# Attention kernel on one core: the chunk mask as two ScalarE copies ahead of the scores, layer 0's output bias in 32-column tiles and added behind the maximum

## The chip, the core and the metric

One core of a Trainium2 chip runs the whole program. Its engines are named as in the profile: PE (TensorE, matmuls), DVE (VectorE), ACT (ScalarE), POOL (GpSimd) and SP (SyncE, which issues the DMAs). PE reads weights and moving data from SBUF and writes PSUM. PE's granted clock was 0.996 of full speed (2.4 GHz) in the profiled execution. The metric is the device time of the program in microseconds, the median of three runs.

## What is computed

Sixteen samples, each 256 channels by 2048 positions, go through two attention layers. `ctx` is y below.

```python
# layer 0: 8 heads of 32 channels; scores over positions, 32x32 for each head
q, k, v = Wq @ y + bq, Wk @ y + bk, Wv @ x + bv
attn = softmax(einsum('bhdl,bhel->bhde', q, k) / 16)
o = Wo @ einsum('bhde,bhel->bhdl', attn, v) + bo + x
x1 = group_norm(o) * gn_w + gn_b          # one mean and variance for each sample
# layer 1: q, k, v from y; chunks of 64 positions, 8 heads
s = einsum('bnqhd,bnkhd->bnhqk', qh, kh) / sqrt(32)
s = s + where(mask_of_key > 0, 0, -1e9)
out = (softmax(s) @ vh) @ W_out.T + b_out
z = out.transpose * mask + x1
return (z - mean) * rsqrt(var + eps)      # over positions, for each channel
```

Layer 0 never forms q, k and v: the kernel builds the Gram matrix of y, from it the scores and the attention, and folds the attention and the weights into one 256x256 matrix M (with the identity added for the residual) and one bias of 256 values. Then o = M x + bias.

## The kernel before

**Slots and units.** A sample is cut in 4 blocks of 512 positions; a block in 4 slots, so a sample has 16 slots s = 0 to 15, with b, j = divmod(s, 4) and u, e = divmod(s, 2). A unit u (0 to 7) is 256 positions, four chunks. Every engine has its own instruction stream, written out by hand in a `body(n, first, last)` that runs over the slots; semaphores alone tie them together. The last sample leaves the loop after slot 11 and has a hand-written tail on PE, ACT and DVE.

**Layer 1.** In each slot PE makes projections of the next block out of y split in a high and a low part (three matmul passes of 128x512 or 128x256 columns, `three_pass`, L313): q and k in slots j = 0 and 1, v in j = 2 and 3. In an even slot `scores(n, u)` writes the unit's scores into `s_ps` (two PSUM banks, one unit deep). It begins with four mask matmuls of 32 rows and 512 columns (L326), which multiply `blocked` (1 where a key is masked, bf16, from `flags` on DVE, L835) with `neg_rows` (-1e9 over the scale, in three bf16 pieces) and open the accumulation, and goes on with 32 small matmuls in 32x64 tiles (L337). DVE takes the maximum (`top`, L839) and subtracts it (`shift`, L846), ACT takes the exponents (L650), DVE sums (L851) and inverts, POOL scales the probabilities (L1125), PE transposes them (L348) in the next two slots, ACT copies that out (L645), and two units later (`LAG` = 2) PE multiplies with v (`values`, L366). ACT casts the result to `att_hi` (L668), DVE makes `att_lo` (L863), PE applies W_out, DVE adds the branch's bias and mask (`branch`, L868). The scores of a unit wait until the `shift` before them has emptied `s_ps`.

**Layer 0.** Slots 1 to 4 build the Gram matrix (`gram_part`, L433), 5 to 8 turn it into scores: `copy_hl` and `copy_lower` on ACT, `L441` to `L465` on PE, the column tiles of L459 and L465 being 32 wide. Slot 10 (`S_U`): DVE normalizes, PE makes U (L471), ACT's `copy_u0` (L707) copies it out after the exponents. Slot 11 (`S_M`): PE makes M (L477) and, on the whole array, the bias W bv (L480, 128x128 weights, one column); DVE adds the identity (L903), splits M in m_hi and m_lo (L905, L907) and adds bo to the bias (L908). In slots 12 to 15 (`S_MX`) PE makes o for a block of x in two halves of six matmuls (`layer0_output`, L313 into `l_ps`), ACT copies each half out with the bias (`copy_output`, L683), DVE takes statistics (L915). x is split by ACT and DVE one slot earlier (`split_x`, L623 and L829), from slot 11 on.

**The sample before.** Its normalization runs under the next sample: ACT's `group_normed` (L658), POOL's `join` (L1142), DVE's statistics and `result` (L994, in slots 10 to 13), SP's stores.

**Order within DVE's slots.** For slots 11 and 12 it is: branch, sums, split_x, result, the three instructions of M, o_bias; then branch, top, att_low, shift. The PE stream of slot 12 is scores(6), values(4), the output of block 0, the projections.

**SP** loads x, y, yt and the mask two to three slots ahead of their use, each load behind a wait until its buffer is free.

## Time and profile before

| | |
|---|---|
| median of three runs | 1559.06 us (1558.3 to 1560.88) |
| profiled execution | 1557.83 us, its span 1556.0 us |
| PE busy | 1527.3 us, 98% |
| DVE busy | 1324.1 us, 85% |
| ACT busy | 999.5 us, 64% |
| POOL busy | 451.4 us, 29% |
| q1, all loads and stores | 32.0% of 16 DMA engines |
| granted clock of PE | 0.996 |

The profile comes from one execution. A group of instructions is named by its line, engine, operation and tiles, out <- in, with shapes; the page's groups give busy time and the mean of one. In a timeline each row is a start, a duration and an instruction; what stands in brackets is the idle time of that engine ahead of it and who ended it. Instructions of one engine overlap a little, so the cost of one is best read from start to start. The chain of work that ended last is followed backwards from the last instruction through whatever released each step. All times of a timeline are microseconds from the start of the span.

### The profile page before, as it was taken

The numbers are of one execution on the slowest core, as the hardware profiler recorded it, in microseconds if no ns is written. First come the engines' busy times: TensorE is split into PE (matmuls) and PEld (weight loads), VectorE is DVE, ScalarE is ACT, GpSimd is POOL, SyncE is SP. The second block draws the span as 40 slices with busy tenths as digits, with TensorE's granted clock in tenths as the row PEclk, the third lists the DMA queues.
The fourth block names the chain that finished last, engine by engine and source line by source line (L and its number), as shares of the span: only waits on it lengthen the run. The fifth ranks groups of instructions, "written<-read, shape, count | busy, mean of one in ns | idle before, by whom it ended". The sixth has DMA issues, their size and how long they took to land.

```text
span 1556.0 us, 55525 instructions
## 1 busy us (share of the span) xinstructions
PE 1527.3 (98%) x24660; PEld 1287.2 (83%) x24660; DVE 1324.1 (85%) x2028; ACT 999.5 (64%) x1808; POOL 451.4 (29%) x294
## 2 busy tenths in 40 slices
PE   9999999999999999999999999999999999999995
PEld 7888888888888888888888888888888888888874
DVE  5778888888898888988888888888888889898897
ACT  5656665666656667566575665766666665666655
POOL 1114133141331414214142241423314133141331
PEclk9999999999999999999999999999999999999998
DMA  7132331424324242241433415234142331424221
GB/s 256 54 96 77 110 123 41 145 84 117 110 67 133 70 142 86 83 123 63 143 83 103 124 45 151 88 98 123 49 150 79 120 111 55 133 82 127 59 72 67
DMA packets 96399, 157.33 MB, mean 101 GB/s; under 512 B 5408, under 2 KB 38304, under 8 KB 96032
## 3 DMA queue, kind: packets, MB, share of 16 engines
q1 hardware_dynamic: 96160, 153.78, 32.0%
q8 instruction: 195, 3.19, 0.9%
q14 instruction: 44, 0.36, 0.1%
HBM read 120.20 MB, written 33.55 MB: 99 GB/s over the span
## 4 chain that ended last, share of the span: by engine, by line
PE 86%; DVE 12%; issue 1%; ACT 1%; POOL 0%; ACTq 0%; POOLq 0%; DVEq 0%
PE pj_ps L313 41%; PE l_ps L313 12%; PE l_ps L433 7%; PE s_ps L337 7%; PE w_ps L348 7%; PE w_ps L366 6%; DVE o_sb L994 3%; PE s_ps L326 2%; PE l_ps L450 2%; DVE row_sum L851 1%; DVE prob L846 1%; DVE x_lo L829 1%; DVE y_lo L820 1%; DVE u_sb L868 1%; DVE m_lo L907 1%
## 5 line engine op out<-in xcount | busy, mean ns | idle before, releaser
L1125 POOL TENSOR_TENSOR prob<-prob,row_inv 128x1024 f32<-128x1024 f32 x128 | 258.3, 2018 | 903.8 <-DVE row_inv L856 903.8
L668 ACT CAST att_hi<-w_ps 128x256 fp32r<-128x256 f32 x256 | 82.9, 376 | 227.4 <-PE w_ps L366 221.0
L313 PE MATMUL pj_ps<-y_hi,w_hi 128*128 128x512 f32 x510 | 206.8, 405 | 0.0
L313 PE MATMUL pj_ps<-y_hi,w_lo 128*128 128x512 f32 x510 | 201.3, 395 | 0.0
L313 PE MATMUL pj_ps<-y_lo,w_hi 128*128 128x512 f32 x510 | 201.2, 394 | 0.0
L851 DVE TENSOR_REDUCE row_sum<-prob 128x16 f32<-128x1024 f32 x128 | 154.9, 1210 | 52.1 <-ACT prob L650 52.1
L839 DVE TENSOR_REDUCE row_max<-s_ps 128x16 f32<-128x1024 f32 x128 | 155.9, 1218 | 33.7 <-PE s_ps L337 31.1
L645 ACT COPY prob_t<-w_ps 128x512 f32<-128x512 f32 x256 | 149.8, 586 | 14.2 <-PE w_ps L348 11.4
L1142 POOL TENSOR_TENSOR o_sb<-o_sb,u_sb 128x1024 f32<-128x1024 f32 x60 | 157.9, 2642 | 2.6 <-ACT o_sb L658 2.6
L824 DVE TENSOR_TENSOR yt_hl<-yt_raw,yt_hl 128x1024 fp32r<-128x1024 f32 x64 | 119.8, 1872 | 42.7 <-ACT yt_hl L613 40.8
L846 DVE TENSOR_TENSOR prob<-s_ps,row_max 128x1024 f32<-128x1024 f32 x128 | 155.4, 1214 | 0.1
L313 PE MATMUL pj_ps<-w_hi,y_hi 128*128 128x256 f32 x512 | 150.3, 294 | 0.7 <-ACT v_s L641 0.7
L348 PE MATMUL w_ps<-cst,prob 128*128 128x128 f32 x1024 | 147.6, 275 | 1.8 <-DVE att_lo L863 1.8
L337 PEld LDWEIGHTS s_ps<-k_s,q_s 32*64 32x64 f32 x8192 | 140.7, 133 | 9.5
L630 ACT ACTIVATE q_s<-pj_ps,col 128x512 f32<-128x512 f32 x128 | 88.3, 690 | 88.0 <-PE pj_ps L313 87.1
L313 PE MATMUL pj_ps<-w_hi,y_lo 128*128 128x256 f32 x512 | 144.6, 282 | 0.0
L313 PE MATMUL pj_ps<-w_lo,y_hi 128*128 128x256 f32 x512 | 144.0, 281 | 0.0
L683 ACT ACTIVATE o_sb<-l_ps,o_bias 128x512 f32<-128x512 f32 x128 | 88.7, 693 | 86.2 <-PE l_ps L313 86.1
L337 PE MATMUL s_ps<-k_s,q_s 32*64 32x64 f32 x8192 | 140.7, 217 | 0.0
L650 ACT ACTIVATE prob<-prob 128x1024 f32<-128x1024 f32 x128 | 137.3, 1072 | 4.7 <-DVE prob L846 4.7
L348 PEld LDWEIGHTS w_ps<-cst,prob 128*128 128x128 f32 x1024 | 118.8, 141 | 24.1 <-issue 10.4
L829 DVE TENSOR_TENSOR x_lo<-x_raw,x_hi 128x1024 fp32r<-128x1024 f32 x62 | 82.2, 1325 | 59.1 <-ACT x_hi L623 59.0
(141 smaller groups left out, 3540.0 us busy)
## 6 DMA issues: line engine op xcount, KB each, us to landing
y_raw<-in_ctx SPq DMA_DIRECT2D x64, 512.0 KB, 4.8
yt_raw<-in_ctx_t SPq DMA_DIRECT2D x64, 512.0 KB, 4.8
x_raw<-in_x SPq DMA_DIRECT2D x64, 512.0 KB, 5.3
out_z<-o_sb SPq DMA_DIRECT2D x60, 512.0 KB, 3.6
mask_b<-in_mask SPq DMA_DIRECT2D x64, 256.0 KB, 4.0
out_z<-o_sb SPq DMA_DIRECT2D x8, 256.0 KB, 2.6
u_sb<-in_w SPq DMA_DIRECT2D x2, 512.0 KB, 5.8
w_sb<-in_w SPq DMA_DIRECT2D x1, 1024.0 KB, 11.1
```

What stands on the lines that cost most here:

```text
L313: last = mm(dst, lhs, rhs, start=i == 0, stop=i == len(todo) - 1)
L337: last = mm(s_ps[64 * h:64 * h + 64, r, t // 2, g, t % 2, :], q_s[rows, b % 2, g, cut], k_s[rows, b % 2, g, cut], start=False, stop=t == 3 ...
L348: last = nc.tensor.transpose(pt_ps[:, j, 2 * g + r, :], prob[:, u % 2, r, j, g, :], ident)
L433: last = mm(l0_ps[i][:, i * P:], yt_hl[:, lb, 0, i * P:(i + 1) * P], hi_lo[:, i * P:], start=q == 0 and lb == 0, stop=q == BLOCKS - 1 and ...
L645: copy(prob_t[:, j].rearrange("p g r h q -> p (g r h q)"), w_ps[:, j, :]).then_inc(pt_copied, 1)
L650: nc.scalar.activation(cut, cut, ACT.Exp, scale=SCALE1).then_inc(exp_done, 1)
L824: tt(yt_hl[:, :, 1, :], yt_raw[:, q % 2], yt_hl[:, :, 0, :], ALU.subtract).then_inc(yt_lo_done, 1)
L839: nc.vector.tensor_reduce(row_max[:, u % 2, :], s_ps[:, :, :, :, :, :].rearrange("p r j g c k -> p (r j g c) k"), AX.X, ALU.max).then_inc( ...
L846: tt(prob[:, u % 2].rearrange("p r j g (c k) -> p (r j g c) k", c=2), s_ps[:, :, :, :, :, :].rearrange("p r j g c k -> p (r j g c) k"), ro ...
L851: nc.vector.tensor_reduce(row_sum[:, u % 2, :], prob[:, u % 2].rearrange("p r j g (c k) -> p (r j g c) k", c=2), AX.X, ALU.add).then_inc(s ...
L1125: nc.gpsimd.tensor_tensor(cut, cut, row_inv[:, u % 2, :].unsqueeze(2).to_broadcast([P, 2 * HEADS, CHUNK]), ALU.mult).then_inc(probs_done, 1)
L1142: nc.gpsimd.tensor_tensor(o_sb[:, :, cut], o_sb[:, :, cut], u_sb[:, :, cut], ALU.add).then_inc(z_done, 1)
```

## The change

The mask matmuls go. `blocked` becomes f32 and holds -1e9 over the scale (or 0) itself; before each unit ACT copies it, spread over the heads, into both banks of `s_ps` (`preset_mask`), and all score matmuls add to what stands there. A copy for unit u + 1 is issued right behind the exponents of unit u and waits for the shift of unit u; PE's scores wait for it. Five zero matmuls instead of six at the start write all of `s_ps` once.

On ACT `copy_lower` moves from slot 7 to slot 6 and `copy_u0` within slot 10, both ahead of the exponents.

Layer 0's bias leaves slot 11: `layer0_bias` makes it as sixteen matmuls in 32-column tiles behind `values(n, 4)` in slot 12, and DVE's `output_bias` adds bo right behind `top(n, 6)`. PE waits for it only ahead of the second half of block 0's output, ACT ahead of its first copy. DVE does the three instructions of M in slot 11 ahead of `result`. In the last sample SP loads x one slot earlier, and DVE's tail takes `top`, the bias and `att_low` ahead of `split_x(n, 1)`.

The diff, without the lines that only declare or drop semaphores and `neg_rows`:

```diff
@@ -96,7 +95,7 @@
         v_s = sb("v_s", [P, 2, PAIRS, E])
-        blocked = sb("blocked", [P, 2, BT], BF16)
+        blocked = sb("blocked", [P, 2, BT])
...
@@ -274,6 +272,8 @@
                         q = s - start + 2
+                        if last and load == load_x:
+                            q += 1
                         if 2 <= q < 6 and not (last and q >= 4):
...
@@ -317,16 +317,7 @@
                     pe.wait_ge(qkv_copied, count(n, 24, 6 * b + 3))
-                    pe.wait_ge(blocked_done, count(n, 4, b))
-                if exists(n, 8, u - 1):
-                    pe.wait_ge(shifted, count(n, 8, u - 1))
-                for i in range(4):
-                    r, h = divmod(i, 2)
-                    rows = slice(DH * i, DH * i + DH)
-                    mm(s_ps[64 * h:64 * h + 64, r].rearrange("p j g c k -> p j g (c k)"), neg_rows[rows, :],
-                       blocked[rows, b % 2, e * UT:(e + 1) * UT].rearrange("p (j t) -> p j t", j=2).unsqueeze(2).to_broadcast([DH, 2, HALVES, P]),
-                       start=True, stop=False)
-
+                pe.wait_ge(mask_set, count(n, 8, u))
...
@@ -335,7 +326,7 @@
                             last = mm(s_ps[64 * h:64 * h + 64, r, t // 2, g, t % 2, :], q_s[rows, b % 2, g, cut], k_s[rows, b % 2, g, cut],
-                                      start=False, stop=t == 3 and g == HALVES - 1)
+                                      start=False, stop=True, skip_group_check=True)
                 last.then_inc(scores_ready, 1)
...
@@ -474,19 +465,27 @@
                         for i in range(HALVES):
-                            mm(l0_ps[0][:, k * E:(k + 1) * E], w0_sb[:, V_W, i, k * P:(k + 1) * P], u0[:, i, :], start=i == 0, stop=i == 1)
-                    for k in range(HALVES):
-                        for i in range(HALVES):
-                            last = mm(l0_ps[1][:, k:k + 1], u0[:, i, k * P:(k + 1) * P], col[:, V_BV0, i:i + 1], start=i == 0, stop=i == 1)
+                            last = mm(l0_ps[0][:, k * E:(k + 1) * E], w0_sb[:, V_W, i, k * P:(k + 1) * P], u0[:, i, :], start=i == 0, stop=i == 1)
                     last.then_inc(m_ready, 1)
+
+            def layer0_bias(n):
+
+                pe.wait_ge(u0_copied, count(n, 1, 0))
+                for k in range(HALVES):
+                    for i in range(HALVES):
+                        for h in range(4):
+                            last = mm(l0_ps[1][DH * h:DH * h + DH, k:k + 1], u0[:, i, k * P + DH * h:k * P + DH * h + DH], col[:, V_BV0, i:i + 1],
+                                      start=i == 0, stop=i == 1)
+                last.then_inc(bias_ready, 1)
...
                     pe.wait_ge(m_lo_done, count(n, 1, 0))
-                    pe.wait_ge(o_bias_done, count(n, 1, 0))
                 for o in range(HALVES):
+                    if q == 0 and o == 1:
+                        pe.wait_ge(o_bias_done, count(n, 1, 0))
                     if exists(n, 8, 2 * q + o - 2):
...
@@ -503,10 +502,9 @@
             zeros = prob[:, 0].rearrange("p r j g m -> p (r j g m)")[:, 0:512]
-            for i in range(6):
+            for i in range(5):
                 last = mm(s_ps[:, i % 2].rearrange("p j g c k -> p (j g c k)"), zeros[:, 0:P], zeros, start=True, stop=True)
             last.then_inc(banks_open, 1)
-            pe.wait_ge(banks_open, 1)
             pe.wait_ge(w_hi_done, 1)
...
@@ -536,6 +533,8 @@
                             values(n, u - LAG)
+                    if s == S_MX:
+                        layer0_bias(n)
                     if s == 0 and not first:
...
@@ -563,6 +562,7 @@
             values(n, 4)
+            layer0_bias(n)
             layer0_output(n, 0)
...
@@ -649,6 +649,19 @@
+            def preset_mask(n, u):
+                b, e = divmod(u, 2)
+                if e == 0:
+                    act.wait_ge(blocked_done, count(n, 4, b))
+                if exists(n, 8, u - 1):
+                    act.wait_ge(shifted, count(n, 8, u - 1))
+                else:
+                    act.wait_ge(banks_open, 1)
+                for r in range(2):
+                    last = copy(s_ps[:, r].rearrange("p j g c k -> p j g (c k)"),
+                                blocked[:, b % 2, e * UT:(e + 1) * UT].rearrange("p (j t) -> p j t", j=2).unsqueeze(2).to_broadcast([P, 2, HALVES, P]))
+                last.then_inc(mask_set, 1)
+
             def group_normed(n, q):
...
@@ -678,6 +691,8 @@
                     act.wait_ge(stored[q], count(n - 1, 1, 0, 16))
+                if q == 0:
+                    act.wait_ge(o_bias_done, count(n, 1, 0))
                 for o in halves:
...
@@ -719,6 +734,7 @@
                 copy_k(0, 0, g)
+            preset_mask(0, 0)
             for m in range(2):
...
@@ -740,8 +756,6 @@
                         copy_hl(n)
-                    if s == S_SUM + 1:
-                        copy_lower(n)
                     if s == S_SC + 1:
...
@@ -758,12 +772,15 @@
                         copy_pt(n, u - 1, 0)
+                    if s == S_SUM:
+                        copy_lower(n)
+                    if s == S_U:
+                        copy_u0(n)
                     if e == 0:
                         exponents(n, u)
+                        preset_mask(n, u + 1)
                     if j == 1 and not (last and b + 2 >= BLOCKS):
                         split_y(n, b + 2)
-                    if s == S_U:
-                        copy_u0(n)
                     if not first and s in (2, 3):
...
@@ -785,6 +802,7 @@
             copy_output(n, 1)
+            preset_mask(n, 7)
             split_x(n, 3)
...
@@ -831,8 +849,8 @@
                 if exists(n, 8, 2 * (b - 2) + 1):
-                    dve.wait_ge(scores_ready, count(n, 8, 2 * (b - 2) + 1))
-                nc.vector.tensor_scalar(blocked[:, b % 2, :], mask_b[:, b % 4, :], 0.0, None, ALU.is_le).then_inc(blocked_done, 1)
+                    dve.wait_ge(mask_set, count(n, 8, 2 * (b - 2) + 1))
+                nc.vector.tensor_scalar(blocked[:, b % 2, :], mask_b[:, b % 4, :], 0.0, NEG / SCALE1, ALU.is_le, ALU.mult).then_inc(blocked_done, 1)
...
@@ -905,7 +923,6 @@
                     tt(m_lo[:, :, :], m_t[:, :, :], m_hi[:, :, :], ALU.subtract).then_inc(m_lo_done, 1)
-                    tt(o_bias[:, :], l0_ps[1][:, 0:HALVES], col[:, V_BO0, :], ALU.add).then_inc(o_bias_done, 1)
                 elif S_MX <= s < S_MX + BLOCKS:
...
@@ -913,6 +930,10 @@
                     nc.vector.bn_stats(o_stats[:, HALVES * q + o, :], o_sb[:, o, q * BT:(q + 1) * BT]).then_inc(o_stats_done, 1)
+
+            def output_bias(n):
+                dve.wait_ge(bias_ready, count(n, 1, 0))
+                tt(o_bias[:, :], l0_ps[1][:, 0:HALVES], col[:, V_BO0, :], ALU.add).then_inc(o_bias_done, 1)
...
@@ -1024,6 +1041,8 @@
                         top(n, u)
+                        if s == S_MX:
+                            output_bias(n)
                         if not (first and u < LAG):
...
@@ -1053,11 +1072,14 @@
                         instance_norm(n - 1)
+                    if s == S_M:
+                        layer0(n, s)
                     if not first and T_FINAL <= s < T_FINAL + BLOCKS:
...
                         layer0_inverse(n)
-                    layer0(n, s)
+                    if s != S_M:
+                        layer0(n, s)
                     if s == SLOTS - 1 and not last:
...
@@ -1066,10 +1088,11 @@
             branch(n, 1, 1)
+            top(n, 6)
+            output_bias(n)
+            att_low(n, 4)
             split_x(n, 1)
-            top(n, 6)
             shift(n, 6)
-            att_low(n, 4)
             split_x(n, 2)
```

## Rows read from the trace of the kernel before

**Rows 1.** Page of the profile: busy time and share by engine; the chain that ended last.

```profile
PE 1527.3 (98%) x24660; PEld 1287.2 (83%) x24660; DVE 1324.1 (85%) x2028; ACT 999.5 (64%) x1808; POOL 451.4 (29%) x294
...
PE 86%; DVE 12%; issue 1%; ACT 1%; POOL 0%; ACTq 0%; POOLq 0%; DVEq 0%
```

**Rows 2.** List of waits: engine, what waited <- releaser: us in total, times, longest.

```profile
PE l_ps L313 <- DVE o_bias L908: 6.3, 14, 0.6
```

**Rows 3.** Timeline of PE, sample 7, slots 11 and 12: start us, us, engine, line.

```profile
744.48 0.95 PE L480 MATMUL l_ps<-col,work_b 128*128 128x1 f32 x8
...
745.29 0.48 PE L313 MATMUL pj_ps<-att_hi,w_hi 128*128 128x512 f32 x1
...
746.86 0.41 PE L326 MATMUL s_ps<-blocked,neg_rows 32*64 32x512 bf16 x4
...
747.10 1.10 PE L337 MATMUL s_ps<-k_s,q_s 32*64 32x64 f32 x64
...
749.59 0.47 PE L313 MATMUL l_ps<-x_hi,m_hi 128*128 128x512 f32 x1 [0.60 <-DVE o_bias L908]
```

**Rows 4.** Groups of ACT by line and shape: busy us, mean ns | idle before.

```profile
L645 ACT COPY prob_t<-w_ps 128x512 f32<-128x512 f32 x256 | 149.8, 586 | 14.2 <-PE w_ps L348 11.4
...
L658 ACT ACTIVATE o_sb<-o_sb,gn 128x512 f32<-128x512 f32 x120 | 91.4, 815 | 0.0
```

**Rows 5.** Timeline of ACT, slots 5, 6, 9 and 10 of sample 7; [idle before it].

```profile
713.83 0.69 ACT L634 ACTIVATE k_s<-pj_ps,col 128x512 f32<-128x512 f32 x1 [0.47 <-PE pj_ps L313]
...
716.22 0.65 ACT L668 CAST att_hi<-w_ps 128x256 fp32r<-128x256 f32 x2 [0.48 <-PE w_ps L366]
...
734.47 0.69 ACT L634 ACTIVATE k_s<-pj_ps,col 128x512 f32<-128x512 f32 x1 [0.53 <-PE pj_ps L313]
...
736.53 0.65 ACT L668 CAST att_hi<-w_ps 128x256 fp32r<-128x256 f32 x2
```

**Rows 6.** Timeline of DVE and GpSimd (POOL), slots 11 and 12 of sample 7.

```profile
743.65 1.16 DVE L829 TENSOR_TENSOR x_lo<-x_raw,x_hi 128x1024 fp32r<-128x1024 f32 x1
...
743.82 2.75 POOL L1125 TENSOR_TENSOR prob<-prob,row_inv 128x1024 f32<-128x1024 f32 x1 [7.80 <-DVE row_inv L856]
...
744.73 2.58 DVE L994 TENSOR_SCALAR o_sb<-o_sb,z_rstd,z_shift 128x512 f32<-128x512 f32 x2
...
747.23 0.68 DVE L903 TENSOR_TENSOR work_a<-l_ps,cst 128x512 f32<-128x512 f32 x1
...
747.94 0.43 DVE L905 CAST m_hi<-work_a 128x512 fp32r<-128x512 f32 x1
...
749.08 0.74 DVE L868 SCALAR_TENSOR_TENSOR u_sb<-pj_ps,c,mask_b 128x512 f32<-128x512 f32 x1
...
750.87 0.74 DVE L863 TENSOR_TENSOR att_lo<-w_ps,att_hi 128x256 fp32r<-128x256 f32 x2
...
755.74 1.00 DVE L994 TENSOR_SCALAR o_sb<-o_sb,z_rstd,z_shift 128x512 f32<-128x512 f32 x2
```

**Rows 7.** GpSimd's scaling on the page's groups; an x_lo of slot 13, timeline of DVE.

```profile
L1125 POOL TENSOR_TENSOR prob<-prob,row_inv 128x1024 f32<-128x1024 f32 x128 | 258.3, 2018 | 903.8 <-DVE row_inv L856 903.8
...
760.68 1.72 DVE L829 TENSOR_TENSOR x_lo<-x_raw,x_hi 128x1024 fp32r<-128x1024 f32 x1 [1.34 <-ACT x_hi L623]
```

**Rows 8.** Chain in order of time, slot 8: start us, us, what.

```profile
730.37 0.39 PE l_ps L459 x32
```

**Rows 9.** Timeline of PE and ACT, slots 10 and 11 of sample 7.

```profile
738.57 1.10 PE L471 MATMUL l_ps<-w_sb,a_wide 128*128 128x256 f32 x4
...
739.65 1.06 ACT L650 ACTIVATE prob<-prob 128x1024 f32<-128x1024 f32 x1 [0.29 <-DVE prob L846]
...
742.01 1.05 ACT L623 CAST x_hi<-x_raw 128x1024 fp32r<-128x1024 f32 x1
```

**Rows 10.** Chain at the start of the span; timeline of ACT in the last sample.

```profile
1.31 7.07 PE s_ps L507 x12
...
1515.33 1.05 ACT L623 CAST y_hi<-x_raw 128x1024 fp32r<-128x1024 f32 x1 [3.39 <-DMA x_raw<-in_x]
```

More of the change, by code:

```diff
@@ L152, in build @@
         wqk_in, wvo_in, cols_in, consts_in, w0_in = sem("wqk_in"), sem("wvo_in"), sem("cols_in"), sem("consts_in"), sem("w0_in")
-        neg_done = sem("neg_done")
-        zeros_set, banks_open = sem("zeros_set"), sem("banks_open")
+        zeros_set, banks_open, mask_set = sem("zeros_set"), sem("banks_open"), sem("mask_set")
         consts_done = sem("consts_done")
@@ L1004, in _ @@
             flags(0, 0)
-            dve.wait_ge(consts_in, 16)
-            for i in range(4):
-                last = nc.vector.tensor_copy(neg_rows[DH * i:DH * i + DH, :], cst[0:DH, C_NEG:C_NEG + CHUNK])
-            last.then_inc(neg_done, 1)
             split_y(0, 1)
```

4 lines of the change are left out of this document (1 added, 3 removed).

## Prediction

> **What bounds the kernel now.** I began with the page: TensorE (PE) is busy for 98% of the span, VectorE (DVE) for 85%, ScalarE (ACT) for 64%, and the chain that ended last runs 86% on PE and 12% on DVE [rows 1]. So what leaves PE comes off the time, except where PE waits. Then the list of waits: in the steady state one wait of PE is left, 0.45 us in each of 14 samples, the first matmul of layer 0's output for the bias (`o_bias`) [rows 2]. Then sample 7 in order of time (one sample takes 95.3 us): before that matmul PE stood 0.60 us [rows 3], and DVE had worked without a break since slot 10. So slots 10 to 12 are set by DVE, all others by PE. I name stretches by their slot, units 0 to 7 by their scores; all times are those of sample 7.
>
> **The mask leaves PE.** Each unit has four mask matmuls, which start at 746.86; the scores behind them start at 747.10 [rows 3]. That is 0.24 us. The chain of PE shows 0.34 for them, since it counts the 0.1 us gap ahead of them too, which is a change of tile size and stays when the scores follow the projections directly. The first weights of the scores, now hidden under the mask, may come into the open; that takes up to 0.07. I take 0.24 us a unit, bounds 0.17 and 0.34.
>
> **Two ACT copies a unit take its place.** The trace has no ACT copy from SBUF to PSUM. The nearest is the copy of 128x512 out of PSUM, 586 ns; the dearest form with 512 columns takes 815 ns [rows 4]. Back to back ACT instructions overlap by about 0.1, so a pair costs 0.96 us, bounds 0.9 and 1.45. In all 128 pairs, 123 us, put ACT at 73% of the span. The pair stands behind the exponents, a whole unit (about 12 us) ahead of its scores, so the scores don't wait for it; what it delays is ACT's queue behind it: the transposed copy, the split of x or yt, k's copies, split_y, and `att_hi`, for which att_lo on DVE and then PE's transposes wait. ACT's idle time takes this up in most slots. Two places are tight. Slots 5 and 6: 0.47 us of idle before k's second copy and 0.48 before `att_hi` just hold a pair [rows 5], but not PE's new earliness too, so unit 3 gains 0.17 instead of 0.24. Slots 9 and 10: 0.53 before k and none before `att_hi` [rows 5], so `att_hi` comes when it came before, and unit 5's mask gives nothing.
>
> The other units: the mean over partitions in slot 0 waits for DVE's aggregate, which comes within 0.3 us of PE now, so unit 0 gains 0.10. Units 7, 1, 2 and 4 gain 0.24 each. Sum: 0.96 + 0.17 + 0.10 = 1.23 us a sample; unit 6 belongs to the next part. The flags now write f32 with a second operation, same columns; DVE has that time.
>
> **Slots 10 to 12, the order of DVE.** Today x_lo is followed by result (2.50 us for two), the sum of M (0.71), m_hi, m_lo and o_bias, which ends at 749.16; PE starts the output at 749.59 and its second half 1.39 later, at 750.98 (half of a group of 2.79) [rows 3, 6]. Result is that slow because GpSimd's scaling of the probabilities came in at 743.82, behind x_lo, and took 2.75 us [rows 6]. The mean over all 128 is 2.02, about 17 of them long, so 1.91 for the others [rows 7]. It and these DVE instructions exclude each other: two results cost 0.91 (755.74 to 756.65) where GpSimd rests, and an x_lo started under a running scaling took 1.72 instead of 1.16 [rows 6, 7].
> After: x_lo leaves DVE at 744.73. The sum of M reads PSUM and runs under the scaling, its input ready at once, since the bias matmuls are no longer ahead of the signal. m_hi, at 745.44, copies from SBUF to SBUF at the speed of a result (0.43 and 0.46 for 512 columns), not of a sum (0.6 to 0.7), so I take it as held as the result was, until the scaling ends at 746.57, and done at 746.78. Then m_lo 0.61 (747.39), two results at their free cost 0.91 (748.30), branch and maximum 1.79 (750.09) [rows 6], and only then o_bias, done at 750.24. m_lo comes in time. The bias comes 1.08 us later than before, because branch and maximum now stand ahead of it, but it is wanted 1.39 later.
> PE on its side: the bias matmuls on the whole array took 0.81 (744.48 to 745.29) [rows 3]; as 32-column tiles they resemble the 32 small ones of y's sums, 0.39 for all [rows 8]; with 0.24 for unit 6, PE would start the output at 748.28 and reach its second half at 749.67. There it waits for o_bias: 750.24 and 0.1 to 0.42 of restart. So the second half starts at 750.34 to 750.66 instead of 750.98, and the bias, the mask and the old wait, worth 1.3 together, give 0.3 to 0.6. I take 0.5. Sum for a sample: 1.73 us.
>
> **x_hi and the port.** copy_u0 is moved ahead of the exponents. Its matmuls end at 739.67 [rows 9], so: copy at 739.71, exponents at 740.18 (before: 739.65), pair at 741.14, transposed copy 742.10, x_hi at 742.58 against 742.01 [rows 9], done at 743.62. x_lo may then start at 743.65, when it starts now, and 0.17 ahead of the scaling. That is the thinnest margin of the change.
> The Trainium skill, SBUF — State Buffer, section Who interferes with whom, says that the first to issue gets the pair of ports shared by DVE and GpSimd for its whole instruction and that the other is blocked; the rows of the scaling agree, and by that rule a pair 0.2 us dearer turns the order round, which is the first rival.
> The Trainium skill, ScalarE: Activation LUTs, gives an ACTIVATE without pointer operands 186 ns + 0.833 ns an element, from which I estimate 0.61 us, and also says that writing to PSUM is quicker than to SBUF; no row here shows it. By 0.61 x_lo starts at 743.71, by a quicker write earlier, ahead of GpSimd in both, and the sum stays.
>
> copy_lower, one slot earlier, finds its transpose done; 0.27 us ahead of exponents that have slack. Ends: PE's chain begins with twelve records (six matmuls) of zeros up to 8.38 us [rows 10]; five end near 7.5 and the weights at 7.91 take over: 0.45, and 0.24 for unit 0. In the last sample ACT stands 3.39 us for x [rows 10]; that load moves one slot ahead on SP's queue, in front of a store, and att_low comes before split_x, but DVE is nearly full there: 1.6, bounds 0 and 2.7.
>
> **Sum.** 15 x 1.73 = 26.0, 0.7 and 1.6: 28.3 us. Profiled execution 1557.83 - 28.3 = 1529.5 (span 1527.7); the median of the three runs lies 1.23 above it, so 1530.8.
>
> **Rivals.**
> (a) GpSimd gets in first. If the pair costs over about 1.15 us, x_lo starts after 743.82, is blocked to 745.73 and leaves DVE at 746.81; then 0.71, 0.46, 0.61, 0.91, 1.79 and 0.15 put o_bias at 751.44, 1.20 later than forecast. 16 x 1.20 = 19: 1550. For: the margin of 0.17. Against: ACT's copies are regular (586 ns on average over 256).
> (b) The bias isn't late. If the cast isn't held by GpSimd, m_lo is done at 746.5, the first result is held as it is now, and o_bias is done at 749.17, 1.07 earlier; PE never waits: 0.81 more a sample, 1518; with masks at 0.34, 1511. For: the sum of the sizes that leave PE. Against: the held result of the same speed [rows 6].
> (c) Slower: the write into PSUM is dear. If a copy of 512 columns costs as much as the longest ACT instruction, 1.06 us for the exponents of 1024 [rows 9], a pair takes 1.93, 0.97 more. It then comes out whole in slots 5 and 6 and again in 9 and 10, and (a) besides: 1.73 - 0.97 - 0.97 - 1.20 = -1.4 us a sample, 1578 with the ends. It turns slower from a pair of about 1.3 us, where (a)'s 1.20 and twice 0.34 have used up 1.73 and the ends; at 815 ns a copy it would be 1564. No row speaks for it but the lack of one; ACT's copies cost 0.82 ns a column whatever the form.
> (d) PE's gain is used up by small waits at many places (ACT and DVE are both fuller): nothing is left, 1558.
>
> **How the numbers follow.** Forecast 0.43, (a) 0.24, (b) 0.20, (c) 0.08, (d) 0.05. The time is the forecast's. The range leaves out (c), (d) and the outermost of (b): 1510 to 1552. A measurement of this kernel can tell 0.2%, about 3 us, from no change. Faster: forecast, (a) and (b), 0.87; same 0.05; slower 0.08.
>
> **What would show it.** Line 326 gone, ACT near 73% with copies into `s_ps` of 0.56 to 0.62 us; in every sample x_lo of slot 11 at 1.16 us and GpSimd's scaling there at 2.75 (forecast), or x_lo over 2 us and the scaling at 1.91 (a); PE idle about 0.7 to 1 us ahead of the second half of the output's first block, released by o_bias. (b) is shown by no such wait and m_hi at 0.43. The period of a sample should be 93.5 us. The forecast is wrong if a new wait on `att_hi` or on line 915's copies appears in PE's list, or if the score matmuls themselves become longer.

## The result, and the profile of the changed kernel

The changed kernel takes 1548.17 us, median of 4 runs (1545.97 to 1549.55), against 1559.15 for the kernel before (4 runs): ratio 0.9924, 95% interval 0.9912 to 0.9936. It is 11 us faster. The forecast said 28 us faster, 1530.8. The sign was right and the time lies in the range, but the size was wrong by a factor of 2.5. Its profiled execution took 1545.97 us with a span of 1544.2, so 11.8 of the span's 1556.0 us went.

The page's busy times and its chain, to be read beside [rows 1]:

```profile
PE 1506.1 (98%) x24530; PEld 1264.6 (82%) x24530; DVE 1287.5 (83%) x2024; ACT 1109.2 (72%) x2064; POOL 451.0 (29%) x294
...
PE 78%; DVE 12%; ACT 7%; issue 2%; DMA 0%; ACTq 0%; POOL 0%; SPq 0%; POOLq 0%; DVEq 0%
```

PE lost 21 us of busy time, the span only 11.8. ACT is at 72% (forecast: near 73) and now has 7% of the chain, where it had 1%. "issue" has 2%, where it had 1%: time in which PE stood although the profile shows nothing that it waited for. PE's list of waits (us in total, times, longest), the answer to [rows 2]:

```profile
PE l_ps L313 <- DVE o_bias L936: 9.3, 13, 0.9
...
PE w_ps L357 <- issue: 2.8, 5, 1.0
...
PE l_ps L477 <- issue: 1.5, 2, 1.2
```

The wait for the bias did not go, it grew from 6.3 to 9.3 us, as the forecast had it (it stands ahead of the second half now). The other two rows have no counterpart in the kernel before, and the forecast has no term for them. PE in slots 11 and 12 of sample 7, to be read beside [rows 3]:

```profile
740.67 1.16 PE L328 MATMUL s_ps<-k_s,q_s 32*64 32x64 f32 x64
...
742.55 0.43 PE L477 MATMUL l_ps<-col,work_b 128*32 128x1 f32 x32
742.91 0.50 PE L313 MATMUL l_ps<-x_hi,m_hi 128*128 128x512 f32 x1
...
745.26 0.50 PE L313 MATMUL l_ps<-x_hi,m_hi 128*128 128x512 f32 x1 [0.69 <-DVE o_bias L936]
```

The line of the mask is gone; the 32 small bias matmuls take 0.36 (742.55 to 742.91; forecast 0.39); the second half stands 0.69 us for `o_bias` (forecast 0.7 to 1). But the scores take 1.16 us instead of 1.10. DVE and GpSimd in the same stretch, beside [rows 6]:

```profile
738.44 1.23 DVE L847 TENSOR_TENSOR x_lo<-x_raw,x_hi 128x1024 fp32r<-128x1024 f32 x1
739.58 0.68 DVE L921 TENSOR_TENSOR work_a<-l_ps,cst 128x512 f32<-128x512 f32 x1
740.30 1.41 DVE L923 CAST m_hi<-work_a 128x512 fp32r<-128x512 f32 x1
741.74 0.69 DVE L925 TENSOR_TENSOR m_lo<-work_a,m_hi 128x512 fp32r<-128x512 f32 x1
742.35 1.00 DVE L1015 TENSOR_SCALAR o_sb<-o_sb,z_rstd,z_shift 128x512 f32<-128x512 f32 x2
743.26 0.74 DVE L886 SCALAR_TENSOR_TENSOR u_sb<-pj_ps,c,mask_b 128x512 f32<-128x512 f32 x1
743.93 1.21 DVE L857 TENSOR_REDUCE row_max<-s_ps 128x16 f32<-128x1024 f32 x1
745.06 0.15 DVE L936 TENSOR_TENSOR o_bias<-l_ps,col 128x2 f32<-128x2 f32 x1
```

```profile
738.51 2.91 POOL L1148 TENSOR_TENSOR prob<-prob,row_inv 128x1024 f32<-128x1024 f32 x1 [7.61 <-DVE row_inv L874]
```

This is the order that the forecast worked out: x_lo gets in ahead of GpSimd (by 0.07 us; 0.17 before), the sum of M (`work_a`) runs under the scaling, `m_hi` is held until the scaling ends (1.41 instead of 0.43), and the two results take 1.00, as they do where GpSimd rests [rows 6]. In samples 0 and 15 alone GpSimd came first and x_lo took 2.58.

To see where the time went I took the starts of the score matmuls of all 128 units. The table has the distance from one unit's start to the next, less the same distance in the kernel before, as the median of samples 1 to 14: a negative number is time won. "0 to 1" is the stretch from unit 0's scores to unit 1's. The columns are the kernels of this document (e1 to e7 are the experiments below); "forecast" is that of the prediction.

```
us          forecast  after    e1     e2     e3     e4     e5     e6     e7
0 to 1        -0.24   -0.16  -0.17  -0.16   0.00  -0.15  -0.15  -0.15  -0.15
1 to 2        -0.24   -0.15  -0.17  -0.15   0.00  -0.15  -0.15  -0.15  -0.15
2 to 3        -0.17   -0.19  -0.19  -0.19   0.00  -0.19  -0.20  -0.20  +0.99
3 to 4        -0.24   -0.12  -0.18  -0.13  +0.01  -0.12  -0.12  -0.12  +0.06
4 to 5         0.00   -0.04  -0.03  -0.01  +0.01  -0.04  -0.03  -0.03  -0.04
5 to 6                -1.05  -0.17  -0.17  -0.89  -1.06  -1.07  -1.07  -0.90
6 to 7                +0.73   0.00  +0.21  +0.55  -0.24  +1.32  +1.56  +1.55
5 to 7        -0.74   -0.32  -0.17  +0.04  -0.34  -1.30  +0.25  +0.49  +0.65
7 to next 0   -0.10   -0.18  -0.18  -0.18   0.00  -0.18  -0.22  -0.22  -0.22
sum           -1.73   -1.16  -1.08  -0.78  -0.33  -2.13  -0.62  -0.38  +1.15
```

(Sums are those of the unrounded medians.) A second mark, from the start of unit 5's scores to the first matmul behind block 0 of the output in slot 12 (below: the end of the block), shows the DVE stretch by itself: 17.64 us before, 17.54 after (medians of samples 1 to 14). It gave 0.10, where the forecast took 0.5.

### The profile page after: what moved, and what is told of

The parts are those of the page before. It is cut to its first block, busy times and chain, and to the rows that moved or that the text cites. A ratio compares the mean times of both kernels' runs of the same rounds, so it can differ in the third digit from the quotient of the medians.

```text
span 1544.2 us, 55594 instructions
## 1 busy us (share of the span) xinstructions
PE 1506.1 (98%) x24530; PEld 1264.6 (82%) x24530; DVE 1287.5 (83%) x2024; ACT 1109.2 (72%) x2064; POOL 451.0 (29%) x294
## 3 DMA queue, kind: packets, MB, share of 16 engines
q8 instruction: 194, 3.18, 0.9%
## 4 chain that ended last, share of the span: by engine, by line
PE 78%; DVE 12%; ACT 7%; issue 2%; DMA 0%; ACTq 0%; POOL 0%; SPq 0%; POOLq 0%; DVEq 0%
PE pj_ps L313 39%; PE l_ps L313 10%; PE l_ps L424 7%; PE s_ps L328 7%; PE w_ps L339 6%; PE w_ps L357 5%; PE l_ps L441 2%; DVE x_lo L847 1%; DVE o_sb L1015 1%; DVE row_max L857 1%; DVE m_hi L923 1%; DVE prob L864 1%; ACT s_ps L661 1%; ACT prob L650 1%; DVE row_sum L869 1%
## 5 line engine op out<-in xcount | busy, mean ns | idle before, releaser
L328 PEld LDWEIGHTS s_ps<-k_s,q_s 32*64 32x64 f32 x8192 | 130.8, 133 | 43.1 <-issue 35.0
L842 DVE TENSOR_TENSOR yt_hl<-yt_raw,yt_hl 128x1024 fp32r<-128x1024 f32 x64 | 94.9, 1483 | 70.0 <-ACT yt_hl L613 70.0
L328 PE MATMUL s_ps<-k_s,q_s 32*64 32x64 f32 x8192 | 148.5, 220 | 0.0
L661 ACT COPY s_ps<-blocked 128x512 f32<-128x512 f32 x256 | 143.1, 603 | 0.0
```

The costliest lines, as they stand in the source:

```text
L328: last = mm(s_ps[64 * h:64 * h + 64, r, t // 2, g, t % 2, :], q_s[rows, b % 2, g, cut], k_s[rows, b % 2, g, cut], start=False, stop=True, ...
L661: last = copy(s_ps[:, r].rearrange("p j g c k -> p j g (c k)"), blocked[:, b % 2, e * UT:(e + 1) * UT].rearrange("p (j t) -> p j t", j=2). ...
```

## The experiments

All are timed in 5 rounds beside the kernel before, which took 1559.8 to 1560.6 us in those rounds.

### One part alone

**e1_nomask**: the kernel before without a mask; it leaves out the masking of the scores (edit shortened, as all below).

```
-  mm(s_ps[...], neg_rows[rows, :], blocked[...], start=True, stop=False)   # 4 a unit
-  mm(s_ps[...], q_s[...], k_s[...], start=False, stop=...)
+  mm(s_ps[...], q_s[...], k_s[...], start=True, stop=True)
```

> The kernel before without any mask: no mask matmuls, no copies in their place, the scores simply overwrite the banks (the mask of the scores is left out). Theory (slots 10 to 12 are set by DVE, the rest by PE, and a mask is worth 0.18 us of PE, as the chain of the changed kernel shows with 1.09 against 0.34 + 0.93): six of eight units come off, 0.18 x 6 x 16 = 17, so 1542 us. Rival (what leaves PE comes off the time): all eight at 0.34, 43, so 1516; or all eight at 0.18, 23, so 1536. If ACT's copies cost nothing, the mask part alone must come out like this one.

Measured 1544.82 us, ratio 0.9902 (0.9889 to 0.9916), where 1542 was expected; two stalls of PE (below) with 2.0 us are in it. Without any preset on ACT and without any mask a unit is 0.17 to 0.19 shorter, not 0.24, and between units 4 and 5 only 0.03. The scores take 1.16 us, and the old wait has grown by 2.3 us:

```profile
740.86 1.16 PE L331 MATMUL s_ps<-k_s,q_s 32*64 32x64 f32 x64
```

```profile
PE l_ps L313 <- DVE o_bias L902: 8.6, 14, 0.7
```

So the mask matmuls are worth 0.18 a unit on PE itself. The parts add up to that: 0.34 in the chain, less the gap of 0.1 that stays, less the 0.06 by which the scores are longer. That these 0.06 are the scores' first weights, as the prediction had it, fits but is not shown by itself. And unit 6 gives nothing as long as DVE sets the end of slot 12.

**e2_mask_alone**: the mask by ACT with its moved copies, the bias as before (matmuls in slot 11 on the whole array, added behind `m_lo`, all of it ahead of the output). The edit stands against the changed kernel.

```
   # PE, slot 11
-  last.then_inc(m_ready, 1)      # behind M
+  mm(l0_ps[1][:, k:k + 1], u0[...], col[...])    # 4 on the whole array
+  last.then_inc(m_ready, 1)
   # DVE, behind m_lo
+  tt(o_bias, l0_ps[1][:, 0:2], col[:, V_BO0, :], ALU.add)
```

> The mask part of the change alone, with the ACT copies, the moved copy_u0 and copy_lower, the five zero matmuls and the earlier load of x; the bias, DVE's order and DVE's tail as before. Theory: units 7, 0 to 4 gain what the changed kernel shows between its scores (0.18, 0.16, 0.15, 0.19, 0.12), 0.8 to 0.9 us a sample, 13 us, less the single stalls seen in the changed kernel, so 1546 to 1551. Rival (the copies on ACT cost more than they bring, and the bias part carried the 11 us): 1556 to 1562.

Measured 1554.40, ratio 0.9965 (0.9953 to 0.9978): between the two. The column e2 agrees with e1 up to unit 6, except 0.05 between units 3 and 4: ACT's pairs cost PE next to nothing in the steady state. From unit 5 to 7 nothing is left of two masks. The first sample lost 1.05 us between units 1 and 2 (below).

**e3_bias_alone**: the bias and the order of DVE, with the old mask and ACT's old order.

```
   # PE: M signals m_ready first; the bias as 32-column tiles, behind the values
+  mm(l0_ps[1][DH*h:DH*h+DH, k:k+1], u0[...], col[...])   # 16, slot 12
   # DVE, slot 11: M ahead of result; o_bias behind row_max
   # ACT: unchanged
```

> The bias part alone: the 32-column tiles in slot 12, the addition behind the maximum, the three instructions of M ahead of the result, DVE's tail; the mask matmuls stay. Theory: only the arrival of o_bias counts, 1.08 us later than before but wanted 1.39 later, so 0.3 to 0.6 us a sample, 5 to 10 us: 1549 to 1554. Rival (what leaves PE comes off the time): 0.42 for the tiles and 0.45 for the old wait, 14 us: 1545.

Measured 1559.66, ratio 0.9997 (0.9988 to 1.0006): no gain. Unit 5 to 6 wins 0.89, unit 6 to 7 gives 0.55 back, since the bias now comes late. The first block of the output ends at 17.30, 0.34 earlier, and samples 1 to 14 win 14 x 0.33 = 4.6 us at their typical length; sample 0 wins 0.5. Stalls of PE (below) take 3.0 of these. The last sample loses 2.7 (ACT stands 5.7 us for the load of x, which has its old place here, where it stood 3.4), the tail 1.1 (PE's last matmul ends 19.12 us behind the last scores instead of 17.76, at a granted clock of 0.66), the start 0.9, whose cause is open. Together the profiled execution is 2.7 us longer than that of the kernel before. My expectation had 0.3 to 0.6 in each of 16 samples and nothing for the rest.

### The order on DVE

**e4_bias_first**: the changed kernel with the two neighbours exchanged.

```
   # DVE, slot 12 (and the same in the last sample)
+  if s == S_MX: output_bias(n)
   top(n, u)
-  if s == S_MX: output_bias(n)
```

> The changed kernel with one edit: DVE adds the bias ahead of the maximum of unit 6 instead of behind it, in the loop and in the tail. Theory (PE's second half waits for o_bias, and that stands behind a maximum of 1.13 us): the wait of 0.7 to 0.9 us goes, PE is then bound by itself, 16 x 0.85 = 13 us less: 1534 to 1537. Rival (the wait goes to the next late step, shift, att_hi or the copies out): less than 4 us, 1544 to 1548.

Measured 1534.68, ratio 0.9844 (0.9830 to 0.9857): the expected time, and some 13 us faster than the changed kernel. The first block ends at 16.57. PE's and DVE's timelines in sample 7:

```profile
738.20 0.50 PE L313 MATMUL l_ps<-x_hi,m_hi 128*128 128x512 f32 x1
...
739.71 0.39 PE L313 MATMUL l_ps<-x_hi,m_hi 128*128 128x512 f32 x1
```

```profile
739.22 0.15 DVE L936 TENSOR_TENSOR o_bias<-l_ps,col 128x2 f32<-128x2 f32 x1
739.29 1.21 DVE L857 TENSOR_REDUCE row_max<-s_ps 128x16 f32<-128x1024 f32 x1
```

The bias is there 0.34 before the second half (739.71) wants it, and no wait for it is left on PE. One instruction of 0.15 us behind one of 1.21 cost 0.97 us a sample.

**e5_result_first**: the changed kernel with result ahead of M again.

```
-  if s == S_M: layer0(n, s)
   if not first and T_FINAL <= s < T_FINAL + BLOCKS: result(n - 1, s - T_FINAL)
-  if s != S_M: layer0(n, s)
+  layer0(n, s)
```

> The kernel after with one order on VectorE undone: in slot 11 result stands ahead of the sum of M again. Theory (slots 10 to 12 are set by VectorE behind GpSimd's scaling; the move of M took the held time off PE's path): x_lo, then two results held until the scaling ends, then m_t 0.68, m_hi 0.43, m_lo 0.69, branch and maximum 1.8, o_bias. m_lo comes about 0.8 us behind PE, o_bias about 0.7 later than after, so the slot's last output matmul is 0.6 to 0.8 later in each of 16 samples: 1558 to 1561, no better than before. Rival (PE has caught up by other ways and the order is worth nothing): 1548.

Measured 1554.40, ratio 0.9966 (0.9953 to 0.9978). The block ends at 18.13, 0.59 later than after (expected 0.6 to 0.8), some 6.5 us in all. So M ahead of result is worth that much. The mechanism was expected, the time was not: 1558 to 1561 was, no better than the kernel before. DVE's and PE's timelines:

```profile
743.75 2.58 DVE L1015 TENSOR_SCALAR o_sb<-o_sb,z_rstd,z_shift 128x512 f32<-128x512 f32 x2
746.26 0.68 DVE L921 TENSOR_TENSOR work_a<-l_ps,cst 128x512 f32<-128x512 f32 x1
746.97 0.43 DVE L923 CAST m_hi<-work_a 128x512 fp32r<-128x512 f32 x1
```

```profile
748.38 0.47 PE L313 MATMUL l_ps<-x_hi,m_hi 128*128 128x512 f32 x1 [1.24 <-DVE m_lo L925]
```

GpSimd's scaling holds whichever SBUF-to-SBUF instruction stands behind x_lo: result (2.58) here, `m_hi` (1.41) in the changed kernel. `m_hi` is held for less, because the sum of M from PSUM has used 0.7 us of the scaling.

**e6_v_before_x**: rival (a) made true in every sample.

```
   # ACT, slot 11
+  copy_v(n, b + 1, j - 2)
   split_x(n, 0)
-  copy_v(n, b + 1, j - 2)
```

> The kernel after with ScalarE's copy of v in slot 11 put ahead of the split of x, so that x_hi comes some 0.7 us later and GpSimd's scaling starts before x_lo in every sample, as rival (a) of the prediction had it. Theory: x_lo is blocked until the scaling (1.9 us) is over, takes over 2 us, leaves VectorE about 1.9 later than now; m_hi is then not held (0.43 instead of 1.29), so o_bias comes 0.9 to 1.2 later: 15 to 19 us, 1563 to 1567. Rival (the order at the shared port is worth nothing, since the held time is only moved from m_hi to x_lo): 1548 to 1552.

Measured 1558.65, ratio 0.9990 (0.9981 to 0.9999). The block ends at 18.37, 0.83 later than after; 10 us in all, less than the 15 to 19 expected. GpSimd, DVE and PE:

```profile
744.23 1.91 POOL L1152 TENSOR_TENSOR prob<-prob,row_inv 128x1024 f32<-128x1024 f32 x1 [7.63 <-DVE row_inv L878]
```

```profile
744.95 2.27 DVE L851 TENSOR_TENSOR x_lo<-x_raw,x_hi 128x1024 fp32r<-128x1024 f32 x1 [0.79 <-ACT x_hi L623]
...
747.85 0.43 DVE L927 CAST m_hi<-work_a 128x512 fp32r<-128x512 f32 x1
```

```profile
751.83 0.50 PE L313 MATMUL l_ps<-x_hi,m_hi 128*128 128x512 f32 x1 [0.94 <-DVE o_bias L940]
```

The mechanism of the rival is right, and the changed kernel is 0.07 us away from it. Its path was also sized right: rival (a) puts `o_bias` 16.84 us behind the start of unit 5's scores, with an `m_hi` that runs free, and it was done at 16.82. The price is 0.83 and not 1.20 because the changed kernel itself has `o_bias` at 15.98, and not at the forecast's 15.64.

**e7_preset_4**: each preset in four copies of 256 columns.

```
-  for r in range(2):  copy(s_ps[:, r], blocked[...])         # 512 columns
+  for i in range(4):  copy(s_ps[:, r, j], blocked[...])      # 256 columns
```

> The kernel after with each preset of the mask in four copies of 256 columns instead of two of 512: the same columns, twice the fixed cost. Theory (ScalarE is tight ahead of att_hi in slots 6 and 10, and x_hi in slot 11 leads GpSimd by under 0.1 us): a preset costs 0.3 to 0.4 us more, units 3 and 5 each lose that, x_lo falls behind GpSimd's scaling in every sample and o_bias comes 0.9 later still: 1.5 to 1.9 us a sample, 1572 to 1578. Rival (ScalarE has room, and only its busy time grows): 1548 to 1552, ScalarE 40 us busier.

Measured 1581.92, ratio 1.0137 (1.0123 to 1.0151): slower than any other, and slower than expected. Yet each preset costs ACT only 0.2 us more (0.98 for two copies in the chain; here 1.21, 707.24 to 708.45). Two places pay: unit 6 to 7, where the order at the port turns round as in e6, and, which I had not expected, unit 2 to 3. ACT, DVE, GpSimd and PE in slot 3 of sample 7:

```profile
707.24 1.30 ACT L663 COPY s_ps<-blocked 128x256 f32<-128x256 f32 x4
```

```profile
711.43 3.43 DVE L844 TENSOR_TENSOR yt_hl<-yt_raw,yt_hl 128x1024 fp32r<-128x1024 f32 x1 [1.97 <-ACT yt_hl L613]
```

```profile
711.41 5.71 POOL L1167 TENSOR_TENSOR o_sb<-o_sb,u_sb 128x1024 f32<-128x1024 f32 x2
```

```profile
715.01 1.87 PE L424 MATMUL l_ps<-yt_hl 128*128 128x512 f32 x8 [1.13 <-DVE yt_hl L844]
```

GpSimd's addition got in 0.02 us ahead of `yt_lo`, which then took 3.43 instead of 1.28 (both medians of samples 1 to 14), and PE stood 1.13 for it. The two places at which I had called ACT tight, ahead of `att_hi`, lost 0.18 (3 to 4) and nothing (4 to 5). ACT's own time was not the danger; a delay of 0.2 us that brings a DVE instruction behind one of GpSimd costs several times its own size.

### The ends

**e8_tail_fill**: e4 with six matmuls that nobody reads where PE waits for the last `att_hi`.

```
   values(n, 7)
+  for i in range(6): mm(s_ps[:, 0], m_hi[:, 0, 0:P], x_hi[:, 0, :], start=True, stop=True)
   wout(n, 3, 0)
```

> The kernel with VectorE's bias ahead of the maximum (1534.7 us, its last projections at a granted clock of 0.74 and 0.84) with six more matmuls of 512 columns, whose result nobody reads, in the 1.6 us in which PE waits for the last att_hi at the end of the span. Theory (the clock falls because PE stands still there, and this is a part of the tail that the change did not gain): the granted clock stays at 1.00 until the last projection, which ends about 1.5 us earlier; the time falls by 1 to 1.5 us, to 1533.2 to 1533.7. Rival (the fall has another cause): same clock, 1534.7.

Measured 1534.51, ratio 0.9833 (0.9819 to 0.9846), against 1534.68 without them. The windows (busy us of PE, PEld, DVE, ACT, POOL, then the granted clock), first of after, then of e8:

```profile
1524.00:1528.00 4.00, 3.08 (x7) 2.48 (x8) 2.85 (x7) 4.00 (x7) 0.00 (x0) 0.57 0.00 0
```

```profile
1513.00:1517.00 4.00, 4.00 (x31) 2.94 (x17) 3.97 (x8) 3.81 (x7) 0.00 (x0) 1.00 0.00 0
```

The first half of this expectation held: with PE busy in the gap the granted clock stays at 1.00, which is 2.4 GHz. In after it fell to its lower level, 1.2 GHz, behind PE's 1.6 us of standing between the last values and the last projection (0.57 is the mean of a window in which it was at both). In e4 PE's last matmul ended 20.11 us behind the last scores, here 18.58. The second half failed: the last computation ends only 0.5 us earlier (29.42 us behind the last scores instead of 29.93), since the chain that ends last runs mainly on DVE there from 1511 us on, and the time does not show it. Standing does not always bring the fall: the kernel before stands for the same 1.60 us and its clock stayed at 1.00, as it did in its two shifted forms (below) and in e7. In the other seven without filler (after, e1 to e6) it fell; in the five with filler (e8 to e12) it never did. Why it falls in one kernel and not in the other is open.

**e9_first_order**: e8 with unit 1's preset in the first sample moved behind the split of yt.

```
+  if first and s == 1: preset_mask(n, 1)       # behind split_yt
   ...
   exponents(n, u)
-  preset_mask(n, u + 1)
+  if not (first and u == 0): preset_mask(n, u + 1)
```

> The kernel with the bias first and the filled tail (1534.5 us), with one preset moved: in the first sample ScalarE sets the mask of unit 1 behind the split of yt instead of ahead of it. Theory (the preset pushed yt_hi 0.8 us back, so that yt_lo fell behind GpSimd's scaling and took 2.67 us instead of 1.16; PE waited for it, 1.06 us between the scores of units 1 and 2): yt_lo takes 1.2 again, the gap is back at its old length less 0.15, and the time is 1.1 us shorter, 1533.4. Rival (the gram is late for another reason): the gap stays, 1534.5.

Measured 1534.80, ratio 0.9836 (0.9822 to 0.9851). The first sample's `yt_lo` in the timeline of DVE, in after and in e9:

```profile
26.82 2.66 DVE L842 TENSOR_TENSOR yt_hl<-yt_raw,yt_hl 128x1024 fp32r<-128x1024 f32 x1 [0.47 <-ACT yt_hl L613]
```

```profile
26.30 1.16 DVE L847 TENSOR_TENSOR yt_hl<-yt_raw,yt_hl 128x1024 fp32r<-128x1024 f32 x1
```

In after GpSimd's scaling had begun at 26.50. The distance from unit 1 to unit 2 is 0.18 below the kernel before, where it was 1.06 above: the place and its cause are shown. In the profiled executions sample 0 is 1.4 us shorter than in e8. The 1.1 us does not appear in the time; e9's four runs lie up to 6 us apart, and the stalls of the next part scatter by more than 1 us.

### Stalls of PE without a releaser

In every kernel so far PE stood still 2 to 10 times for 0.35 to 2.1 us inside a run of small matmuls, with no semaphore to wait for. In the kernel before alone it never did. PE of after in sample 6, and the DMA queues from 625 to 626 us, where the one packet of 16 KB starts in the third slice (625.05):

```profile
625.51 0.82 PE L357 MATMUL w_ps<-prob_t,v_s 64*32 64x64 f32 x60
...
627.29 0.30 PE L357 MATMUL w_ps<-prob_t,v_s 64*32 64x64 f32 x4 [0.96 <-issue]
```

```profile
q8 instruction: 1, 0.02, 5.8%
```

The page counts 194 such packets, 3.18 MB, in the whole of after: 16 KB each, for 49,751 instructions that PE recorded, one packet for 256. I counted PE's records at each stall. **e10_wait_64**, **e11_wait_128** and **e12_wait_192** shift the stream of e9:

```
   last.then_inc(banks_open, 1)       # behind the zero matmuls
+  for i in range(64): pe.wait_ge(zeros_set, 1)     # 128, 192; true already
```

> The kernel e9_first_order with 64 more instructions in TensorE's stream, all at its start: waits that are true already, passed while the zero matmuls run. Nothing else changes. Theory (the stalls of PE with no releaser, none before and five to ten in every changed kernel, lie where its instruction number passes a multiple of 256, which is one fetch of 16 KB on the queue of instructions, in or behind a stretch of small matmuls, and PE resumes 1.3 to 1.6 us after that fetch has landed): the stalls leave their places and stand at the same instruction numbers modulo 256, so 64 instructions earlier in the program; their sum, now about 6 to 8 us, becomes another, anything from 0 to 12 us, and the time moves with it. Rival (stalls belong to places in the work, or to the traffic of data): same places, same time within 1 us.

> As the one with 64 waits, with 128: by the theory the stalls move to yet other places, again at the same numbers modulo 256, and the time moves with their sum by up to some us; by the rival the same places and the same time within 1 us.

> As the one with 64 waits, with 192: by the theory the stalls move again, and over the four positions (0, 64, 128, 192) the differences of the times follow the sums of the stalls; by the rival all four agree within 1 us.

And **e13_before_wait_64**, **e14_before_wait_128** shift the kernel before in the same way:

> The kernel before with 64 waits that are true already at the start of TensorE's stream, so that its fetches of instructions fall elsewhere. If the change brought the stalls: PE shows no stall without a releaser and the time stays within 1 us of the kernel before. If the kernel before was lucky: some stalls at instruction numbers that are the same modulo 256, and 2 to 6 us more.

> The same with 128 waits: no stall and the same time within 1 us if the change brought the stalls; stalls at other places of the work and 2 to 6 us more if it was luck.

Stalls over 0.35 us within the scores, values and bias tiles of the profiled execution (record number: of the matmul that came late; us since landing: of the latest packet of instructions):

```
kernel        time     stalls  sum us  instruction   us since     some record numbers
                                       modulo 256    landing
before      1559.15       0     0
after       1548.17       7     5.7    193, 194      1.31-1.57    8048 9942 16507
e8          1534.51      10     8.5    193, 194      1.31-1.59    8048 9942 16507
e9          1534.80       6     7.5    193, 194      1.30-1.47    9562 9942 16507
e10 (64)    1535.10       9     7.3    193, 194      1.25-1.56    6517 8032 14977
e11 (128)   1536.47      10     8.6    193, 194      1.25-1.54    4987 6501 13446
e12 (192)   1540.26       6     5.4    193, 194      1.29-1.50    3456 10148 11916
e13 (64)    1562.81       3     2.6    193, 194      1.28-1.45    5002 13085 20788
e14 (128)   1563.02       3     2.4    193, 194      1.39-1.56    3471 3851 11554
```

All 54 stalls of the table stand at the same instruction number modulo 256 and end 1.25 to 1.6 us after a packet landed, in seven different programs of PE. (What is counted is the distance from one matmul's start to the next within a run of one kind.) Records are missing or joined (64 added waits are 32 more records, and the stall at 8048 is at 8032, 16 matmuls of two instructions earlier), but the number modulo 256 is that of the fetch whatever the work is. The theory of e10 to e12 holds in that. The part that the times follow the sums is not shown. e12 is the slowest with the smallest sum, but at its start PE stood 3.54 us behind the zero matmuls, where the 192 waits are (that they took this time is the likely reading), and then worked at a granted clock of 0.76 from 12 to 14 us and of 0.50 from 14 to 16, so that its first scores start 5.1 us later than those of e9:

```profile
11.82 0.48 PE L378 MATMUL pj_ps<-y_hi,w_hi 128*128 128x512 f32 x1 [3.54 <-issue]
```

Without these 5.1 us it would take about 1535.2, and the four times would lie within 1.7 us, less than the runs of e9 do by themselves. The last pair settles the question that was open: ratios 1.0016 (1.0007 to 1.0025) and 1.0011 (1.0002 to 1.0020), about 2 us slower, with three stalls each and every distance between scores otherwise as before (PE's waits in e13):

```profile
PE w_ps L366 <- issue: 2.0, 3, 1.1
```

So the kernel before was lucky by some 2 us. Of after's 5.7, about 3 belong to the change: without the mask matmuls and with 32 more small ones the run in which PE takes 256 instructions in under 2 us is denser. The shares of 3 and 2 rest on three positions of one kernel, and why such a run suffers is argued from these numbers; a kernel with other runs was not tried.

## Why the prediction was wrong in size, by its own steps

Its 28.3 us were 0.7 at the start, 15 times 1.73, and 1.6 at the end. The two profiled executions, compared in the same pieces:

```
                                 forecast   measured
start (first scores)                0.7        0.4     (0.1 to 0.6 in e1, e2, e4 to e7)
sample 0                            1.7       -0.1
samples 1 to 14, typical           24.2       16.2     (14 x 1.16)
   less stalls                                -3.0
sample 15 and the tail              1.6       -1.6
sum                                28.3       11.9
```

The missing 16.4 us are thus 8.0 in the typical sample (14 x 0.57: 0.40 in slots 10 to 12, 0.17 in the masks), 3.0 in stalls, 3.2 in the last sample and the tail, 1.8 in sample 0 and 0.3 at the start.

- **What bounds the kernel**: right. Slots 10 to 12 are set by DVE, all others by PE; e1 shows both (0.17 to 0.19 at the other units, and nothing at unit 6).
- **Mask, 0.24 a unit**: mis-sized; 0.18 lies inside its bounds (0.17 to 0.34). The term "up to 0.07" for the first weights was what it measured, 0.06 (scores of 1.16 instead of 1.10), and it was left out of the sum. Longer score matmuls were one of the prediction's own signs that it is wrong. Seven units were to give 1.23 and gave 1.06: unit 0 gave more (0.18, not 0.10), units 1, 2 and 4 less. That unit 5 gives nothing came out (0.04), but e1 has the same 0.03 without a single preset on ACT: it is not the pair that takes it. What does is open.
- **ACT's pair, 0.96 us**: right, 0.98 in the chain. The copies stand in the list of groups, to be read beside [rows 4]:

```profile
L645 ACT COPY prob_t<-w_ps 128x512 f32<-128x512 f32 x256 | 152.2, 596 | 3.9 <-PE w_ps L339 3.0
L661 ACT COPY s_ps<-blocked 128x512 f32<-128x512 f32 x256 | 143.1, 603 | 0.0
```

  They agree with the estimate that the prediction made from the Trainium skill, ScalarE: Activation LUTs, section What ACT_TABLE_LOAD costs: 0.61 us. A quicker write to PSUM does not stand out: 603 ns from SBUF to PSUM, 596 from PSUM to SBUF. Since the two also read from different memories, they don't settle it.
- **Slots 10 to 12, 0.5 a sample**: this is the step that failed most, 0.10 (17.64 to 17.54), which over 15 samples is 6 of the 16.4 us missing. The mechanism was right, down to the order of the instructions and the one that is held; the size of the win was not. Counted from the start of unit 5's scores, the bias was forecast done at 15.64 and the second half at 15.88 (0.5 before 16.38); measured 15.98 and 16.05. Three small things make up the 0.4. The second half came 0.17 later: the scaling took 2.91 us, not 2.75, and `m_hi` was done 0.3 later than in the sum, of which PE gave some back by starting 0.05 behind the bias, and not 0.1 to 0.42. Sample 7 of the kernel before had the longest of its waits, 0.60, where twelve of the 14 were 0.43: the old second half stands at 16.27 in the median, and not at 16.38 (16.43 in sample 7 by the row itself, 751.03, where the prediction took half of a group), so there was 0.11 less to gain. And from the start of the second half to the end of the block it took 1.49 with the wait in front of it, and 1.37 without, 0.13 more.
- **x_hi and the port**: right that x_lo stays ahead in nearly all samples, by a margin that shrank from 0.17 to 0.07. The step looked at one place. The same turn happened at a place that it did not look at, `yt_lo` of the first sample (1.2 us of the missing 1.8 there; e9). A held instruction costs nothing where PE does not wait for it: in the kernel before two of the four `yt_lo` of a sample took 2.94 and 2.19 us in the median (2.11 and 1.28 after), and e1, where they are as long as before, wins as much between its scores.
- **Ends, 2.3 us**: wrong in sign for the end, and 0.4 for 0.7 at the start (the first projection came 0.54 earlier, at 7.88 us, the first scores 0.41). The load of x, forecast at 1.6, gave about 0.5 (between units 6 and 7 the last sample is at +0.19, the typical one at +0.73). It was issued 0.07 us behind the x_lo that frees its buffer, where it had stood 3.0 behind it, but this x_lo was one of the two that GpSimd held (2.58), and ACT still waits for the load, 2.83 us where it was 3.39 [rows 10]. The tail from the last scores on took 34.8 us instead of 32.7; PE's last matmul ends 2.2 later: 0.8 before the last output block (0.5 of it a stall) and 1.4 in the last projection at the fallen clock.
- **Stalls**: no step had them; about 3 us by the change and some 2 that the kernel before had been spared.
- **Rivals**: (a) was shown as a mechanism (e6), not met; (b) came true only in e4, by another order; (c) fell with 603 ns a copy, but it was cheap as it was worked out: it has the change turn slower from a pair of about 1.3 us, and e7's pair of 1.21 already gave 1582, since the rival did not have `yt_lo`; of (d) something is in the ends and in the stalls.

## What to carry to other kernels

A sum that is worked out in one sample should use the median of all samples for the wait that it removes (0.43 here, where the chosen sample had 0.60), and a term whose bound is a known loss ("up to 0.07") belongs in the sum. A stretch set by DVE beside GpSimd should be read at the ends of GpSimd's instructions, at all places where a delayed engine feeds DVE; and a small instruction that PE waits for is worth moving ahead of the big one beside it (0.15 ahead of 1.21: 13 us here). A forecast of 1 to 2% for a kernel whose PE runs at 98% needs a term of some us for fetches of instructions (5.4 to 8.6 us of stalls in six of the eight kernels counted, 2.4 and 2.6 in two).

## What the runs showed of the hardware

- PE gets its instructions in packets of 16 KB, one for 256 of them; in runs of small matmuls (256 instructions in about 2 us) it can stand 0.4 to 2.1 us at the border, until 1.25 to 1.6 us after the packet has landed. A shift of the stream by 32 to 64 instructions alone made the kernel before about 2 us slower.
- GpSimd's 1.9 us scaling takes 2.9 when x_lo is ahead of it, and a DVE instruction from SBUF to SBUF that starts behind a GpSimd one takes until that ends (`yt_lo` 3.43 and 2.66 instead of 1.16; `m_hi` 1.41 instead of 0.43), while the sum that reads PSUM keeps its 0.68 (e5 and after). The prediction cited the Trainium skill, SBUF — State Buffer, section Who interferes with whom, for the first to issue holding the ports; the trace agrees, down to margins of 0.02 to 0.07 us.
- An ACT copy from SBUF to PSUM cost 389 ns for 256 columns (e7) and 603 for 512; a preset in four such copies cost 0.2 us more than in two.
- Dropping a matmul in front of a change of tile size moves part of its time into the next ones: the four mask matmuls had 0.34 in the chain and gave 0.17 to 0.19 between scores (e1).
- Six matmuls that nobody reads, in a gap of 1.6 us, kept PE's granted clock at 1.00, and the last matmul ended 1.5 us earlier than in e4, where the mean granted clock of the last projection was 0.63 (e8 and e4).
